# Layer 0's cross attention with the scoring rounds of one batch set between the attending rounds of another, two banks at a time

## The reference

```
q, k, v  = h @ Wq, h @ Wk, h @ Wv          # h = layernorm(x); q and k are rotated (rope)
w        = softmax(q k^T / sqrt(8) + attention_mask)
a_k, a_v = adapter @ Wk, adapter @ Wv      # adapter = ctx, 128 positions
out      = w v + tanh(gate) * softmax(q a_k^T / sqrt(8)) a_v
x        = x + out @ Wo
```

## Time and profile before

| | |
|---|---|
| median of 3 runs | 4114.19 us (4107.68 to 4115.82) |
| profiled execution, its own time | 4105.98 us |
| its span | 4104.2 us |
| PE busy in the span | 3288.6 us (80%) |
| DVE, ACT busy | 2604.6 us (63%), 1760.3 us (43%) |
| the changed stage, first PE record to last DVE record | 127.98 to 775.3 us |

### The profile page before, as it was taken

One profiled execution on the slowest core, in us unless ns is written; L12 is line 12 of the kernel. 1 busy time (PEld: TensorE's weight loads), 2 busy tenths in 40 slices (PEclk: granted clock), 3 DMA queues, 4 the chain that ended last, 5 costly groups with the idle time before them and its releaser, 6 DMA issues. The chain is left out here.

```text
span 4104.2 us, 79104 instructions
## 1 busy us (share of the span) xinstructions
PE 3288.6 (80%) x29375; PEld 2408.5 (59%) x29376; DVE 2604.6 (63%) x6900; ACT 1760.3 (43%) x3973; POOL 110.0 (3%) x125
## 2 busy tenths in 40 slices
PE   7777777444687988988998995587996799778999
PEld 6555555211464656656656664466886677545788
DVE  6544545588686776776776766776882288476133
ACT  2344343377344666666666664223432244220011
POOL 2000000000000000000000000000100000000000
PEclk9999999655898999999999998797888999888699
DMA  2000000000400000000000002000000000142100
GB/s 91 22 21 20 16 20 15 1 0 0 149 21 3 2 1 3 1 1 3 1 1 3 1 1 89 1 0 16 15 11 0 0 1 0 31 107 57 43 11 10
DMA packets 85656, 81.26 MB, mean 20 GB/s; under 512 B 12528, under 2 KB 78704, under 8 KB 84848
## 3 DMA queue, kind: packets, MB, share of 16 engines
q1 hardware_dynamic: 84288, 77.68, 6.3%
q10 hardware_dynamic: 1200, 1.11, 0.1%
HBM read 76.67 MB, written 2.11 MB: 19 GB/s over the span
## 5 line engine op out<-in xcount | busy, mean ns | idle before, releaser
L2991 PE MATMUL bank<-L1w_w,L1x_xqT 128*128 128x512 f32 x640 | 304.3, 599 | 2.1 <-DVE L1x_xqT L3246 2.1
L3054 PE MATMUL bank<-L1w_wp,L1x_catT 128*128 128x256 f32 x1024 | 244.0, 381 | 12.0 <-ACT L1x_catT L3162 12.0
L1042 ACT ACTIVATE L0x_P<-bank,L0x_level 128x512 f32<-128x512 f32 x256 | 155.1, 688 | 187.5 <-PE bank L992 187.5
L3252 DVE TENSOR_REDUCE L1x_ssq<-L1x_square 128x4 f32<-128x512 f32 x192 | 131.5, 685 | 148.2 <-ACT L1x_square L3124 143.8
L3156 ACT ACTIVATE L1x_cat<-bank,L1x_osum 128x128 f32<-128x128 f32 x512 | 146.4, 368 | 170.5 <-DVE L1x_osum L3283 170.5
L3054 PEld LDWEIGHTS bank<-L1w_wp,L1x_catT 128*128 128x128 f32 x1024 | 186.8, 190 | 49.2 <-ACT L1x_catT L3162 15.0
L1058 DVE TENSOR_REDUCE L0x_top<-bank 128x4 f32<-128x512 f32 x256 | 159.0, 684 | 72.9 <-PE bank L970 71.1
L3039 PE MATMUL bank<-L1x_v,L1x_PT 128*128 128x129 f32 x1024 | 147.2, 286 | 65.5 <-ACT L1x_PT L3151 65.5
L3013 PEld LDWEIGHTS bank<-ident,L1x_hat 128*128 128x128 f32 x768 | 91.6, 144 | 151.7 <-DVE L1x_hat L3262 115.2
L3134 ACT ACTIVATE L1x_hatT<-bank,L1w_affine 128x512 f32<-128x512 f32 x192 | 148.7, 774 | 70.4 <-PE bank L3013 68.4
L3124 ACT ACTIVATE L1x_square<-bank 128x512 f32<-128x512 f32 x192 | 115.6, 602 | 133.9 <-PE bank L2991 133.9
(11 more groups left out here) (649 smaller groups left out, 7902.0 us busy)
## 6 DMA issues: line engine op xcount, KB each, us to landing
L0x_mask<-in_maskrows SPq DMA_DIRECT2D x16, 512.0 KB, 3.7
L3w_wg<-in_L_ffn_Wg SPq DMA_DIRECT2D x8, 704.0 KB, 8.5
L3w_wu<-in_L_ffn_Wu SPq DMA_DIRECT2D x8, 704.0 KB, 9.4
L1w_wp<-in_L_xattn_wproj SPq DMA_DIRECT2D x1, 4096.0 KB, 29.9
L3x_ctxT<-in_ctxT SPq DMA_DIRECT2D x32, 128.0 KB, 2.1
L3w_wd<-in_L_ffn_Wd SPq DMA_DIRECT2D x8, 512.0 KB, 8.7
L0x_ctxT<-in_ctxT SPq DMA_DIRECT2D x16, 128.0 KB, 2.1
L1w_w<-in_L_xattn_wq SPq DMA_DIRECT2D x1, 2048.0 KB, 9.7
```

What stands on the lines that cost most here:

```text
L1042: act.activation(self.P[:, i % 2, r, :], self.work_bank[r][:, :], ACT.Exp, bias=self.level[:, :]).then_inc(self.p_ready.sem, 1)
L2991: last = pe.matmul(made_bank[n % 4][:, :], inputs(SOURCE[n], k), w[:, k, 4 * n:4 * n + 4, :], start=(k == 0), stop=(k == C - 1))
L3054: last = pe.matmul(y_bank[:, 0:D], catT[:, j, :], wp[:, 4 * m + j, :], start=(m == 0 and j == 0), stop=(m == MG - 1 and j == 3))
L3252: dve.tensor_reduce(ssq[:, 4 * n:4 * n + 4], square[:, n % 2, :].rearrange("p (h e) -> p h e", h=4), X, ALU.add).then_inc(sum_ready.sem, 1)
```

## The change

The stage is put in another order, on all engines.

- The scoring round i of batch b+1 is followed, after other work of PE, by the attending round i of batch b, in the same four banks: scoring waits (`score_free`) for the exponentials of the attending round before it, attending (`shift_free`) for the maxima of the scoring round before it.
- Both rounds are done in two halves (`PAIRS`): banks 2 and 3 with the row groups 0 and 1, then banks 4 and 5 with the row groups 2 and 3, each half with its own wait, mask included.
- Keys, values, queries, masks and contexts stand in three sets (`SETS`) instead of two; the loop (`ring_of_three`) has three turns, is run 4 times, and there is one more turn at the end, in which the last batch's fourth mix, its output transpose and its projection with wo are done (`behind`).
- The projection of the context's keys goes to the second half of bank 0 instead of bank 6, the transposed maxima to banks 0 and 1; the projections stand at other places of the turn, and DVE's rotations, normalizations and the residual between its maxima. The number of matmuls per batch stays the same.

```diff
-    MADE = 6
+    PAIRS = ((0, 1), (2, 3))
+    SETS = 3
+    MADE = 2 * SETS + 2
...
-        self.top_out = self.out_bank[:, 0:D].bitcast(BF16)
-        self.y_out = self.out_bank[:, D:2 * D]
+        self.top_out = [kit.bank[s][:, 0:128].bitcast(BF16) for s in range(2)]
+        self.y_out = self.out_bank[:, 0:D]
...
         s, c = divmod(i, C)
-        if i >= 1:
-            pe.wait_ge(self.top_found.sem, self.top_found.after(b, 4 * i))
-        if s == 0:
-            self.mask_tensor(pe, mask)
-        for r in range(self.ROWS):
-            rows = self.rows_of(r)
-            pe.matmul(self.work_bank[r][:, :], self.qT[odd][rows, c, :], self.kM[odd][s][rows, c, :, :],
-                      start=(s == 1), stop=True).then_inc(self.scored.sem, 1)
...
+        for some in self.PAIRS:
+            wait_free(i, some[-1])
+            if s == 0:
+                self.mask_tensor(pe, mask, some)
+            for r in some:
+                rows = self.rows_of(r)
+                pe.matmul(self.work_bank[r][:, :], self.qT[n][rows, c, :], self.kM[n][s][rows, c, :, :],
+                          start=(s == 1), stop=True).then_inc(self.scored.sem, 1)
...
-        if i >= 1:
-            pe.wait_ge(self.p_ready.sem, self.p_ready.after(b, 4 * i))
-        else:
-            pe.wait_ge(self.top_found.sem, self.top_found.after(b))
...
-        for j in range(self.SLOTS):
-            for r in range(self.ROWS):
-                rows = self.rows_of(r)
-                pe.matmul(self.work_bank[r][:, j * 128:(j + 1) * 128], self.kM[odd][s][rows, c, j, :], self.qT[odd][rows, c, :],
-                          start=(s == 1 and j == 0), stop=False)
...
+        for some in self.PAIRS:
+            wait_free(i, some[-1])
+            if s == 0:
+                self.mask_tensor(pe, mask_T, some)
+            for j in range(self.SLOTS):
+                for r in some:
+                    rows = self.rows_of(r)
+                    pe.matmul(self.work_bank[r][:, j * 128:(j + 1) * 128], self.kM[n][s][rows, c, j, :], self.qT[n][rows, c, :],
+                              start=(s == 1 and j == 0), stop=False)
+            for j in range(self.SLOTS):
+                for r in some:
+                    rows = self.rows_of(r)
+                    last = pe.matmul(self.work_bank[r][:, j * 128:(j + 1) * 128], self.select[rows, j:j + 1].to_broadcast([32, 128]),
+                                     self.topT[rows, i, :], start=False, stop=(j == self.SLOTS - 1))
+                    if j == self.SLOTS - 1:
+                        last.then_inc(self.shifted.sem, 1)
...
+def ring_of_three(eng, turn):
+
+    for b in range(-2, 1):
+        turn(b, b % 3, b)
+    with eng.Fori(0, (B - 4) // 3) as t:
+        for i in (1, 2, 3):
+            turn(t * 3 + i, i % 3, i)
+    for b in range(B - 3, B + 1):
+        turn(b, b % 3, b)
+
...
+                def score_free(i, r):
+                    if here and i >= 1:
+                        pe.wait_ge(at.p_ready.sem, at.p_ready.after(b, 4 * (i - 1) + r + 1))
+                    elif behind:
+                        pe.wait_ge(at.p_ready.sem, at.p_ready.after(b - 1, 12 + r + 1))
+                    elif here:
+                        pe.wait_ge(at.top_found.sem, at.top_found.after(b, 12 + r + 1))
+                    elif i >= 1:
+                        pe.wait_ge(at.top_found.sem, at.top_found.after(b + 1, 4 * (i - 1) + r + 1))
+
+                def shift_free(i, r):
+                    if ahead:
+                        pe.wait_ge(at.top_found.sem, at.top_found.after(b + 1, 4 * i + r + 1))
+                    elif i >= 1:
+                        pe.wait_ge(at.p_ready.sem, at.p_ready.after(b, 4 * (i - 1) + r + 1))
+                    else:
+                        pe.wait_ge(at.p_ready.sem, at.p_ready.after(b - 1, 12 + r + 1))
...
+                if ahead:
+                    scores(0)
+                if entering:
...
+                    turn_tensor(kit, pe, bank[0], kit.xn)
+                    project_T(pe, bank[0][:, D:2 * D], wk, ctxT[:, enter_n, :, :]).then_inc(turned.sem, 1)
+                if behind:
+                    at.mix_tensor(pe, b - 1, behind_n, 3)
+                if here:
+                    shifts(0)
+                if behind:
+                    at.turn_raw_tensor(pe, b - 1, 3)
...
+                        pe.wait_ge(v_ready.sem, v_ready.after(b + 1))
+                    at.turn_top_tensor(pe, b, 1)
+
+                if ahead:
+                    scores(1)
+                if here:
+                    at.mix_tensor(pe, b, here_n, 0)
+                if behind:
+                    pe.wait_ge(at.o_part.sem, at.o_part.after(b - 1))
+                    turn_tensor(kit, pe, at.out_bank, at.o).then_inc(at.o_turned.sem, 1)
+                if here:
+                    shifts(1)
...
+                    pe.wait_ge(ck_ready.sem, ck_ready.after(b + 2))
+                    project_T(pe, bank[0], wk, kit.xnT)
+                    project_T(pe, bank[0][:, D:2 * D], wkr, kit.xnT).then_inc(k_made.sem, 1)
+
+                if ahead:
+                    scores(2)
+                if here:
+                    at.mix_tensor(pe, b, here_n, 1)
+                if behind:
+                    pe.wait_ge(at.oT_ready.sem, at.oT_ready.after(b - 1))
+                    project(kit, pe, at.y_out, at.oT, wo).then_inc(y_made.sem, 1)
+                if here:
+                    shifts(2)
+                    if behind:
+                        pe.wait_ge(y_read.sem, y_read.after(b - 1))
+                    at.turn_raw_tensor(pe, b, 0)
+                if entering:
+                    if here:
...
                     project_T(pe, bank[1][:, D:2 * D], wqr, kit.xnT).then_inc(q_made.sem, 1)
+
                 if ahead:
-                    pe.wait_ge(q_ready.sem, q_ready.after(b + 1))
-                    pe.wait_ge(k_ready.sem, k_ready.after(b + 1))
-                    pe.wait_ge(ck_ready.sem, ck_ready.after(b + 1))
-                    pe.wait_ge(mask_loaded.sem, mask_loaded.after(b + 1))
-                for i in range(at.ROUNDS):
-                    if ahead:
-                        at.scores_tensor(pe, b + 1, 1 - odd, i, mask[:, 1 - odd, 0, :, :])
-                    if i == 0 and entering:
-                        pe.wait_ge(normed.sem, normed.after(b + 2))
-                        turn_tensor(kit, pe, bank[0], kit.xn).then_inc(turned.sem, 1)
...
-                    if i == 2 and ahead:
-                        if here:
-                            pe.wait_ge(y_read.sem, y_read.after(b))
-                        at.turn_top_tensor(pe, b + 1, 0)
-
-            staged(pe, turn)
+                    scores(3)
+                if here:
+                    at.mix_tensor(pe, b, here_n, 2)
+                if ahead:
+                    if entering:
+                        pe.wait_ge(kT_ready.sem, kT_ready.after(b + 2))
...
+                if here:
+                    at.turn_raw_tensor(pe, b, 1)
+                    shifts(3)
+                if entering:
+                    pe.wait_ge(q_ready.sem, q_ready.after(b + 2))
+                    project(kit, pe, bank[1][:, 0:D], kit.xnT, wv)
+                    project(kit, pe, bank[1][:, D:2 * D], ctxT[:, enter_n, :, :], wv).then_inc(v_made.sem, 1)
+                if here:
+                    at.turn_raw_tensor(pe, b, 2)
...
+                    leaving.first(dve)
                 if ahead:
-                    heads_of(b + 1, 1 - odd)
```

More of the change, by code:

```diff
@@ L933, in constants_pool @@
     def constants_pool(self, pool):
-        v = self.v[0] + self.v[1]
+        v = sum(self.v, [])
         for t in v:
@@ new lines, in load_mask, with replace @@
+            def load_mask(b, n):
+                sp.dma_start(mask[:, n:n + 1, :, :, :], dram["maskrows"][bass.ds(b, 1)].rearrange("a p i c n -> p a i c n")).then_inc(mask_loaded.sem, 16)
+            def replace(b, n):
+                sp.wait_ge(ctx_loaded.sem, ctx_loaded.after(b + SETS - 1))
+                sp.sem_inc(turns, 1)
+                sp.wait_ge(v_made.sem, v_made.after(b))
+                sp.sem_inc(turns, 1)
+                load_context(b + SETS, n)
+                sp.wait_ge(mask_loaded.sem, mask_loaded.after(b + SETS - 1))
+                sp.sem_inc(turns, 1)
+                sp.wait_ge(at.shifted.sem, at.shifted.after(b, 8))
+                sp.sem_inc(turns, 1)
+                load_mask(b + SETS, n)
@@ L1146, in _ @@
+            for b in range(SETS):
+                load_context(b, b)
+                sp.wait_ge(ctx_loaded.sem, ctx_loaded.after(b))
+                load_mask(b, b)
+                sp.wait_ge(mask_loaded.sem, mask_loaded.after(b))
+            times = (B - SETS) // SETS
+            with sp.Fori(0, times) as t:
+                for i in range(SETS):
+                    replace(t * SETS + i, i)
+            for b in range(times * SETS, B - SETS):
+                replace(b, b % SETS)
         @block.tensor
@@ L1165, in turn @@
```

(23 more changed lines are left out.)

262 lines of the change are left out of this document (116 added, 146 removed).

## The result

| | median us | runs, us | ratio to the kernel before |
|---|---|---|---|
| kernel before | 4114.43 | 4107.68 to 4115.82, 6 runs | 1 |
| kernel after | 4139.05 | 4127.80 to 4159.23, 6 runs | 1.0068, 95% interval 1.0044 to 1.0093 |
| kernel after, once more (before: 4108.22) | 4132.87 | 4122.75 to 4139.18, 4 runs | 1.0060, interval 1.0039 to 1.0081 |

The change made the kernel 0.6 to 0.7% slower, about 25 us of 4114. The forecast was 4136 us.

What follows compares the result with a forecast made beforehand. PE was taken as the bound, with turns of 40.0 us. Turns, jumps and half-speed stretches +19.3, fill +5.4 and loads -3 gave +22 us, forecast 4136 us against the median; 8-in-10 range 4095 to 4175.

Steps and rivals of the forecast that it cites:

- The sum: Whole kernel: turns, jumps and half-speed stretches +19.3, fill +5.4, loads ahead -3, together +22 us.
- Work of a plain turn: PE in a plain turn: 28.9 us before, plus 8.5 for masked halves and 2.5 for unmasked attending, gives 39.9.
- Period: Length of a turn, set by PE's work as the bound: 40.0 us, between 39.6 and 41.
- No overlap across a change of shape: Masked rounds: halves of mask and product do not pass each other, +8.5 us per batch.
- Half B of attending without mask: Unmasked attending rounds: half B waits for its maxima, costing 1.28 us each, +2.5 for two rounds.
- Waits gone: PE's waits for exponentials, residual and copies nearly gone, PE busy for 97% or more of the stage's middle.
- rival 3: DVE comes late for maxima and waits return: +1 to +2 us a turn, 4150 to 4162 us; chance 0.10.
- Jumps and clock: Loop jumps at 1.9 us, three instead of six (5.7 against 11.3); half-speed stretches 2 us instead of about 7.
- my 11.3 + 7: Kernel before, its 13 turns: 11.3 us for six loop jumps and about 7 us for half-speed stretches.
- Fill, loads ahead: Stage's start: one more masked scoring round, turn and projection of x, +5.4 us; half B's loads going ahead, -3.
- Rival 1: Masked rounds' halves pass each other across a change of shape: turns of 31.7 us, about 4028 us; chance 0.13.

Runs made afterwards that it cites:

- second profile of after: The kernel after, unchanged, profiled once more for the start of its stage: span 4126.8 us, next stage at 800.19.
- the kernel with one shape: Kernel after with the mask block as one 32 by 128 matmul per row group, output not the reference's: 4045.36 us, ratio 0.9848.
- the kernel with masks together: Kernel after with both halves' masks issued ahead of both products in masked rounds: 4075.69 us, ratio 0.9920.
- written out: Kernel before with its stage's loop written out turn by turn and nothing else changed: 4095.12 us, ratio 0.9961.
- the masked rounds whole: Kernel after with rounds with a mask done for all four banks together, the others in halves: 4072.20 us, ratio 0.9906.

## Why the forecast held, step by step

The direct comparison uses the second profile of after, without the long half-speed stretch: the stage ends 800.19 - 776.25 = 23.9 us later. The sum had +22. By the times, whose medians lie 24.6 us apart (4139.05 - 4114.43), it is the same.

- **Work of a plain turn:** 39.9 forecast, 39.58 measured. The start was set 0.5 too low, 28.9 where the window has 29.44, and the waits with it 0.6 too high, so the rise is 10.1 and not 11, against 8.2 us of waits. The blocks: masked scoring 4.16 and 4.15, masked attending 4.66 and 4.67, attending without mask 2.59 and 2.50. Period 40.0 forecast, 39.8 measured. That a block's time goes with its columns and not its matmuls, read from the earlier trace rows, carried the whole forecast: the mask block lasts 1.14 us with 32 records, 1.09 with 16 and 1.13 with 4 (343.55, the kernel with one shape).
- **No overlap across a change of shape:** right, and borne out by the two kernels that put blocks of one shape side by side. The reason I had, that loads of a new shape waited, was the right one to look at.
- **Half B of attending without mask:** the size was right and the cause half of it. It starts with half A's first shift even when its banks are long free, as in the kernel with masks together; the maxima need not be late for it.
- **Waits gone:** right; exponentials, residual and copies are below 1 us each over the stage. DVE and ACT had the room that I gave them (19.93 and 15.60 of 39.86), so rival 3 did not come.
- **Jumps and clock:** mis-sized, 7.7 us forecast for after, the jumps 5.7 of it. In the second profile the 12 turns from 185.59 to 675.66 take 490.07 us; less 12 x 39.8 that is 12.5, and in the first 494.28 - 477.6 = 16.7, which is 4.2 to 5.6 a jump. Over its neighbours' 39.8 us the six turns with a jump last 4.7, 6.6, 4.5 and 6.3, 4.7, 1.7 us more. The last one is the jump that I had priced at 1.9; behind the other five come half-speed blocks, which I had taken to vanish with the idling. The turn with the last jump (second profile):

```profile
554.62:596.14 41.52, 39.62 (x558) 25.07 (x557) 19.93 (x49) 15.58 (x31) 0.00 (x0) 1.00 0.07 19
```

  For before, my 11.3 + 7 = 18.3 was the measured length less 13 plain turns; written out, the kernel gave back 18.2, so all of it goes with the jumps.
- **Fill, loads ahead:** +5.4 and -3. Left for them are 23.9 - (490.07 + 39.8 - 508.4) = +2.4, the forecast's 2.4. That the two are right one by one is not shown.

The error of 5 to 9 us in the jumps was made good in part by the period: 13 x 0.2 = 2.6. That the sum came so near has luck in it. Rival 1, halves that pass each other, was no idle thought: with one shape for mask and products the masks do in scoring rounds, and that kernel ran at 4045, with turns of 34.9 and not the rival's 31.7, because in attending rounds half B still waits for the first shift.

## What to carry over

Ask of a block of small tiles how many columns stream through each tile: a block on half of the tiles, each with as many columns, takes as long as the whole one. Halves can be had without loss only where they overlap, and here blocks of different tile shape did not. Put those of one shape side by side (both masks, then both products), or leave the block whole: the two came out alike, 0.9920 and 0.9923 of the time before. A change that removes nearly all waits can still lose: compare what PE newly works with what it had waited, here 10.1 us against 8.2 a turn.

## What the runs showed of the hardware

- PE took the first matmuls of half B's mask ahead of half A's scores, which stood before them in the program and waited for their own tile (in the kernel with one shape all eight mask records had started before the first scores at 340.30). But no block of half B started before half A's first bf16 shift. Whether its type, its place behind eight products (16 records), or what it reads does that stays open; no run told them apart.
- In the profiled execution of after PE had no idle time from 163 to 203 us and ran at a granted clock of 0.50 throughout, that is at 1.2 GHz:

```profile
165.76 1.96 PE L959 MATMUL bank<-L0x_mask,ident 32*32 32x512 f32 x16
167.65 2.08 PE L972 MATMUL bank<-L0x_kM,L0x_qT 32*128 32x512 f32 x4
...
206.36 1.14 PE L972 MATMUL bank<-L0x_kM,L0x_qT 32*128 32x512 f32 x8
```

  Before it PE had waited 1.1 us; in the second profile of the same kernel, after the same work, it ran at full speed there. It cost 203.46 - 185.59 = 18 us. What decided between the two is open.
- In the two profiles of after, the six jumps leave PE idle for 1.2 to 1.7 us, though it is otherwise 99% busy. Half-speed blocks follow five of them and cost more than the idling; the sixth has none and its turn is 1.7 us longer. In the kernels with masks together and with the mask in the products' shape the idling is as long (1.2 to 1.6 us), turns across a jump are 1.9 to 2.9 us longer, and no half-speed block follows any of the six. With the masked rounds whole, one jump of three is followed by them (turn of 40.9 us at a clock of 0.92), the others not (38.0 and 38.1 at 1.00). So neither the kernel nor the length of the idling settles it; what does is open.
